# Where the four packed transposes of a gated attention layer land in PSUM: a change of bank and of order

## The chip, the cores and the metric

The kernel runs on one core of a Trainium2 chip. The metric is device time in microseconds (us) of one execution, as the median of several runs. The core's engines run side by side and meet only at semaphores: TensorE (PE in the profile; PEld are its weight loads), VectorE (DVE), ScalarE (ACT), GpSimd (POOL) and SyncE (SP), which only issues transfers here. PSUM has eight banks of 128 x 512 float32; PE writes its results there, DVE and ACT read them.

## The reference

The layer has two halves. The first convolves outer products of a context with a kernel of taps and multiplies with the normalised input; the second is a gated linear attention with two experts per head. Cut to what matters:

```
kv  = einsum('bhil,bhjl->bijhl', ctx, ctx)
out = causal_conv(kv, ssm_kernel) + kv * D
x   = x + tanh(g0) * einsum('bijhl,bhil->bjhl', out, layernorm(x))

y = silu(y_prev * conv_w[:, 0] + y * conv_w[:, 1])      # y = layernorm(x)
q, k, v, g = silu(y @ Wq), y @ Wk, y @ Wv, y @ Wg        # rotary on q and k
q_exp = q * masked_scores * norm ; k_exp = k * onehot    # router from v
o = normalise(tril(q_exp @ k_exp.T) @ v)
x = x + tanh(g1) * (silu(g) * o) @ Wout
```

Shapes: x is (16, 256, 512), float32; 16 heads in the attention.

## The kernel before, in words

The 256 rows of x are cut into 32 groups (`NH`) of 128 rows (8 channels of 16 batches). A Python loop, fully unrolled, runs steps `h = -2 .. 32`. In one step three groups are in flight: `pre` prepares group h+2 (context products `kv` on POOL, their high parts on ACT at L479, their low parts on POOL at L629), `front` convolves group h+1 (`conv`, `conv_last`, then `add_transposed` at L276, 32 transposes that sum `z_terms` into bank 2, from which DVE makes `x2` at L855 and its statistics), `back` projects group h (q, k, logits, v, gate), and `tail` finishes the group whose `back` ran one step earlier (attention output, gate, output projection). Matrix products are made in three passes from a high and a low part of each operand. `back` runs in 32 steps, h = 0 to 31; `tail` in h = 1 to 32; `front` ends with h = 30.

There is no scheduler: the order on each engine is the order in which its block is written, and every hand-over is a `wait_ge` on a semaphore. The part around the change, in PE's order within a step: the v projection into bank 4 (L406); `add_transposed` into bank 2 (L410); the four transposes of `gated` into bank 7 (L415); the gate's projection into bank 5 (L419); the eight transposes of `qke`, k's half into bank 5 (L422) and q's half into bank 3 (L423); the output projection into bank 6 (L432); the scores (L347), which write banks 2, 4, 5 and 3; and, at the head of the next step, the transposes of `z` into bank 7 (L356).

Who reads these banks: ACT applies SiLU to the gate out of bank 5 (L583, `gate_sb`), and copies `gatedT_high` out of bank 7 (L577), k out of bank 5 (L597, `keT`) and q out of bank 3 (L600, `qeT`). DVE makes `gatedT_low` out of bank 7 (L870), behind the chain of `x2` (L855 to L866) in its own order. The layer norm's `rstd2` is made on POOL (L635) and used by ACT for `z` (L590), which stands ahead of the copies of k and q in ACT's order.

Because k's half goes into the bank from which the gate is still to be read, PE waits for `gate_ready` ahead of L422.

Of the kernel before, what the change touches and what calls it, by code (L numbers as in the profile page):

```python
# [13 lines left out]
P = 128  # L14
# [15 lines left out]
def flamingo_gated_layer(nc, x, ctx_t, g_xattn, g_ffn, ssm_kernel, ssm_D, conv_w, Wq, Wk, Wv, Wg,  # L30
# [14 lines left out]
    CH = L // P  # L45
# [20 lines left out]
    with ExitStack() as stack:  # L66
# [195 lines left out]
        def _(eng):  # L262
# [59 lines left out]
            def step(t, p, q, tail, back, front, pre):  # L322
# [14 lines left out]
                def scores():  # L337

                    eng.wait_ge(keT_sb, h + 1)
                    eng.wait_ge(qeT_sb, h + 1)  # L340
                    if front:
# [10 lines left out]
                if back:  # L352
                    eng.wait_ge(z_ready, h + 1)
                    if can_wait(h - 1):
                        eng.wait_ge(gatedT_ready, h - 1)
                    transpose4(bank[7], lambda c: z[:, c * P:(c + 1) * P], zT_ps)  # L356
# [46 lines left out]
                if back:  # L403
                    if can_wait(h):
                        eng.wait_ge(o_normed, h)
                    project(bank[4], yT_p, w_all_p, V0, DV, v_ps, y_low, h + 1)  # L406
                if front:
                    if pre:
                        eng.wait_ge(qx_ready, h + 3)
                    add_transposed(h + 1)  # L410
                if tail:
                    eng.wait_ge(gated_ready, h)
                    if back:
                        eng.wait_ge(y_conv, h + 1)
                    transpose4(bank[7], lambda c: gated[:, c * P:(c + 1) * P], gatedT_ps)  # L415
                if back:
                    if can_wait(h):
                        eng.wait_ge(mask_done[2], h)
                    project(bank[5], yT_p, w_all_p, G0, DV, g_ps, y_low, h + 1)  # L419
                    eng.wait_ge(qke_ready, h + 1)  # L420
                    eng.wait_ge(gate_ready, h + 1)
                    transpose4(bank[5], lambda c: qke[:, RH + 4 * c:RH + 4 * c + 4, :], keT_ps)  # L422
                    transpose4(bank[3], lambda c: qke[:, 4 * c:4 * c + 4, :], qeT_ps)  # L423
                if tail:
                    if isinstance(h, int) and h == 1:
# [13 lines left out]
        def _(eng):  # L439
# [41 lines left out]
            def step(t, p, q, tail, back, front, pre):  # L481
# [83 lines left out]
                if back:  # L565
# [3 lines left out]
                    eng.activation(v_sb[:, :], bank[4][:, :], ACT.Copy).then_inc(v_copied, 1)  # L569
                if pre:  # L570
                    kv_round(p, 2, h + 2)
                    kv_round(p, 3, h + 2)
                if tail:
                    eng.wait_ge(gatedT_ps, h)
                    if can_wait(h - 1):
                        eng.wait_ge(out_ps, h - 1)
                    eng.activation(gatedT_p[0][:, :, :], bank[7][:, :].rearrange("p (c n) -> p c n", c=CH), ACT.Copy  # L577
                                   ).then_inc(gatedT_high, 1)
                if back:
                    eng.wait_ge(g_ps, h + 1)  # L580
# [11 lines left out]
                if back:  # L592
                    eng.wait_ge(keT_ps, h + 1)
                    if can_wait(h):
                        for r in range(CH):
                            eng.wait_ge(attn_ps[r], h)
                    eng.activation(keT[:, :, :], bank[5][:, :].rearrange("p (c n) -> p c n", c=CH), ACT.Copy  # L597
                                   ).then_inc(keT_sb, 1)
                    eng.wait_ge(qeT_ps, h + 1)
                    eng.activation(qeT[:, :, :], bank[3][:, :].rearrange("p (c n) -> p c n", c=CH), ACT.Copy  # L600
                                   ).then_inc(qeT_sb, 1)

            run(eng, step)
# [333 lines left out]
```

## Time and profile before

| | us |
|---|---|
| three runs: lowest, median, highest | 1014.01, 1015.58, 1015.77 |
| the profiled execution's own time | 1016.0 |
| its span, first to last instruction | 1014.2 |
| PE busy in it | 930.4 |
| DVE, ACT, POOL busy | 627.9, 426.9, 672.9 |
| mean granted TensorE clock | 0.981 |

The span is shorter than the execution's time by 1.8 us, which lie around it. A matmul in the timeline is drawn with its modelled duration, which overlaps the next one; the distance between the starts is what PE spends on it. A weight load overlaps the matmul ahead. In a row of the timeline the bracket at the end gives the idle time ahead of the group and who ended it.

### The profile page before, as it was taken

The page shows a single profiled execution, that of the slowest core. Times are in us where ns is not written, and L with a number is a line of the kernel's source. Part 1 is how long each engine was busy: PE and PEld are TensorE (multiplying, and loading weights), DVE is VectorE, ACT ScalarE, POOL GpSimd, SP SyncE. Part 2 cuts the span into 40 slices and gives each one's busy share as a digit, 9 for nine tenths or more (in the row PEclk, how much of TensorE's full clock was granted, in tenths as well). Part 3 has the DMA queues.
Part 4 walks back from the last instruction along what each step waited for, and adds up shares of the span by engine and source line. Part 5 has one row for each costly group of instructions (what it writes and reads, how often), then busy time and mean ns, then how long its engine had stood idle before and what let it go on. Part 6 is the DMA issues. An engine that isn't in the chain of part 4 may idle for free.

```text
span 1014.2 us, 18862 instructions
## 1 busy us (share of the span) xinstructions
PE 930.4 (92%) x7168; PEld 790.7 (78%) x7168; DVE 627.9 (62%) x1400; ACT 426.9 (42%) x906; POOL 672.9 (66%) x613
## 2 busy tenths in 40 slices
PE   1599999999999999999999999999999999999983
PEld 1488888888888888888888888888888878888862
DVE  4766666657666665666666567666656756656542
ACT  2454444444444444434444443444444444444220
POOL 6677667777666677766667776666777666676321
PEclk9889999999999999999999999999999999999986
DMA  8101222112222210222221022222101222210000
GB/s 275 59 30 44 58 58 58 28 31 58 59 58 58 58 32 28 57 59 58 58 58 32 28 57 59 58 59 58 37 24 56 58 59 58 58 37 9 9 12 21
DMA packets 25992, 52.50 MB, mean 52 GB/s; under 512 B 2544, under 2 KB 3696, under 8 KB 25904
## 3 DMA queue, kind: packets, MB, share of 16 engines
q1 hardware_dynamic: 22304, 46.59, 17.1%
q10 hardware_dynamic: 3600, 4.72, 1.4%
q8 instruction: 57, 0.93, 0.4%
q14 instruction: 31, 0.25, 0.1%
HBM read 42.75 MB, written 8.55 MB: 51 GB/s over the span
## 4 chain that ended last, share of the span: by engine, by line
PE 81%; DMA 5%; issue 4%; POOL 4%; DVE 3%; ACT 2%; SPq 0%; POOLq 0%; ACTq 0%
PE bank L315 34%; PE bank L289 19%; PE bank L276 10%; PE bank L265 8%; DMA x_in<-in_x 4%; PE bank L301 3%; PE bank L347 3%; PE bank L333 3%; ACT gate_sb L583 2%; POOL o_rstd L635 1%; DMA w_all<-in_L_ffn_Wv 1%; POOL rstd L635 1%; POOL rot_b L658 1%; DVE gated L827 0%; POOL kv_low L629 0%
## 5 line engine op out<-in xcount | busy, mean ns | idle before, releaser
L629 POOL TENSOR_TENSOR kv_low<-kv,kv_high 128x576 fp32r<-128x576 f32 x128 | 182.0, 1433 | 162.2 <-ACT kv_high L479 162.2
L289 PE MATMUL bank<-kv_high,toep 128*128 128x512 f32 x640 | 225.2, 409 | 11.0 <-DVE z_terms L732 5.6
L620 POOL TENSOR_TENSOR kv<-kx 128x512 f32<-128x512 f32 x128 | 159.2, 1244 | 6.7 <-DMA const<-shape_consts 6.7
L289 PEld LDWEIGHTS bank<-kv_high,toep 128*128 128x128 f32 x640 | 123.0, 192 | 42.1 <-DVE z_terms L732 12.1
L635 POOL TENSOR_TENSOR o_rstd<-o_ve,minus_half 128x16 f32<-128x16 f32 x32 | 93.1, 2911 | 81.7 <-DVE o_ve L802 81.7
L479 ACT ACTIVATE kv_high<-kv 128x576 fp32r<-128x576 f32 x128 | 87.6, 687 | 101.8 <-POOL kv L623 101.8
L289 PE MATMUL bank<-kv_low,toep 128*128 128x512 f32 x320 | 127.4, 398 | 0.0
L315 PE MATMUL bank<-w_all_high,yT_high 128*128 128x512 f32 (+2 forms) x512 | 120.5, 357 | 1.8 <-DVE gated L827 1.8
L880 DVE TENSOR_TENSOR out_sb<-bank,x 128x512 f32<-128x512 f32 x32 | 22.1, 692 | 159.0 <-PE bank L315 159.0
L276 PEld LDWEIGHTS bank<-const,z_terms 128*128 128x128 f32 x1024 | 113.8, 141 | 5.5 <-ACT qx L468 1.2
L276 PE MATMUL bank<-const,z_terms 128*128 128x128 f32 x1024 | 117.0, 273 | 1.0 <-ACT qx L468 1.0
L315 PE MATMUL bank<-w_all_low,yT_high 128*128 128x512 f32 (+2 forms) x512 | 112.7, 342 | 0.0
L315 PE MATMUL bank<-w_all_high,yT_low 128*128 128x512 f32 (+2 forms) x512 | 106.7, 341 | 0.0
L742 DVE TENSOR_TENSOR qke<-rot_a,sel 128x1024 f32<-128x1024 f32 x32 | 69.1, 2158 | 38.8 <-POOL rot_a L661 38.8
L315 PEld LDWEIGHTS bank<-w_all_low,yT_high 128*128 128x128 f32 x512 | 84.4, 190 | 11.1
L315 PEld LDWEIGHTS bank<-w_all_high,yT_low 128*128 128x128 f32 x512 | 81.7, 190 | 11.6
L737 DVE TENSOR_TENSOR att<-bank,const 128x512 f32<-128x512 f32 x128 | 79.5, 684 | 17.8 <-PE bank L347 17.8
L728 DVE TENSOR_TENSOR z_terms<-bank,qx 128x512 f32<-128x512 f32 x128 | 85.4, 667 | 4.5 <-PE bank L289 4.5
L315 PEld LDWEIGHTS bank<-w_all_high,yT_high 128*128 128x128 f32 x512 | 79.2, 191 | 9.0 <-DVE gated L827 3.1
L635 POOL TENSOR_TENSOR rstd<-ve,minus_half 128x1 f32<-128x1 f32 x64 | 36.6, 572 | 69.0 <-DVE ve L793 60.4
L495 ACT ACTIVATE y_raw<-bank,w_conv 128x128 f32<-128x128 f32 x128 | 36.6, 370 | 95.7 <-PE bank L265 95.7
L623 POOL TENSOR_TENSOR kv<-kx 128x64 f32<-128x64 f32 x128 | 73.1, 571 | 0.0
(101 smaller groups left out, 1650.5 us busy)
## 6 DMA issues: line engine op xcount, KB each, us to landing
toep<-taps_dram SPq DMA_DIRECT2D x32, 512.0 KB, 7.1
kx<-in_ctx SPq DMA_DIRECT2D x32, 384.0 KB, 7.5
x_in<-in_x SPq DMA_DIRECT2D x32, 256.0 KB
out_x<-out_sb SPq DMA_DIRECT2D x32, 256.0 KB
w_all<-in_L_ffn_Wv ACTq DMA_DIRECT2D x1, 1024.0 KB, 12.6
w_all<-in_L_ffn_Wg ACTq DMA_DIRECT2D x1, 1024.0 KB, 11.3
w_out<-in_L_ffn_Wout ACTq DMA_DIRECT2D x1, 1024.0 KB, 17.1
router<-in_L_ffn_router_w ACTq DMA_DIRECT2D x1, 512.0 KB, 7.3
```

Source lines behind the costliest of these rows:

```text
L265: ins = nc.tensor.transpose(dst[:, c * P:(c + 1) * P], src(c), ident)
L276: ins = nc.tensor.matmul(bank[2][:, c * P:(c + 1) * P], z_terms[:, c, i * ROW:(i + 1) * ROW], ident, is_transpose=True, start=(c == 0 and ...
L289: ins = nc.tensor.matmul(bank[lc % 2][:, :], toep[:, 1 - p, a, (lc - mc) * P:(lc - mc + 1) * P], kv_p[b][:, 1 - p, mc, 0:FULL], start=(mc ...
L315: ins = nc.tensor.matmul(dst[:, 0:cols], src_p[a][:, c, :], w_p[b][:, c, c0:c0 + cols], start=(i == 0 and c == 0), stop=(i == len(PASSES) ...
L479: eng.activation(kv_p[0][:, p, c, :], kv[:, c % 2, :], ACT.Copy).then_inc(kv_high[c], 1)
L620: eng.tensor_tensor(view(kv[:, c % 2, 0:FULL], [[ROW, NROT], [1, ROW]]), view(kx[:, p, c, 0:ROW], [[0, NROT], [1, ROW]]), view(kx[:, p, c, ...
L623: eng.tensor_tensor(kv[:, c % 2, FULL:FULL + HALF], kx[:, p, c, 0:HALF], kx[:, p, c, HALF:2 * HALF], ALU.mult).then_inc(kv_made[c], 1)
L629: eng.tensor_tensor(kv_p[1][:, p, c, :], kv[:, c % 2, :], kv_p[0][:, p, c, :].bitcast(F32), ALU.subtract).then_inc(kv_ready[c], 1)
L635: eng.tensor_tensor(dst[:, 0:n], src[:, 0:n], minus_half[:, 0:n], ALU.pow).then_inc(done, 1)
L728: eng.tensor_tensor(view(z_terms[:, lc, 0:1], [[ROW, NROT], [1, ROW]]), view(y[:, 0:1], [[ROW, NROT], [1, ROW]]), view(q, [[NB, NROT], [1, ...
L737: eng.tensor_tensor(att[:, r, :, :], bank[SCORE_BANKS[r]][:, :].rearrange("p (c n) -> p c n", c=CH), view(mask[:, 0:1], [[0, CH], [1, P]]) ...
L742: eng.tensor_tensor(view(qke[:, 0, 0:1], [[RATIO * HDK, 2 * RH], [HDK, RATIO], [1, HDK]]), view(rot_a[:, 0, 0:1], [[HDK, 2 * RH], [0, RATI ...
```

## The change

The transposes of k go into bank 7 instead of bank 5. PE does the transposes of `gated` ahead of `add_transposed`, and those of q ahead of those of k. The wait for `gate_ready` moves from the transposes to the scores (which write bank 5); in its old place stands nothing for q, and for k a wait for `gatedT_ready`, after which bank 7 has been read out. The transposes of `z` now wait for `keT_sb` of the step before. ACT copies `gatedT_high` ahead of its last two rounds of `kv_high`, and q ahead of k. No instruction is added or taken away.

```diff
@@ PE @@
                 def scores():
+                    eng.wait_ge(qeT_sb, h + 1)
                     eng.wait_ge(keT_sb, h + 1)
-                    eng.wait_ge(qeT_sb, h + 1)
+                    eng.wait_ge(gate_ready, h + 1)
...
                 if back:
                     eng.wait_ge(z_ready, h + 1)
-                    if can_wait(h - 1):
-                        eng.wait_ge(gatedT_ready, h - 1)
+                    if can_wait(h):
+                        eng.wait_ge(keT_sb, h)
                     transpose4(bank[7], lambda c: z[:, c * P:(c + 1) * P], zT_ps)
...
                     project(bank[4], yT_p, w_all_p, V0, DV, v_ps, y_low, h + 1)
+                if tail:
+                    eng.wait_ge(gated_ready, h)
+                    if back:
+                        eng.wait_ge(y_conv, h + 1)
+                    else:
+                        eng.wait_ge(keT_sb, h)
+                    transpose4(bank[7], lambda c: gated[:, c * P:(c + 1) * P], gatedT_ps)
                 if front:
                     if pre:
                         eng.wait_ge(qx_ready, h + 3)
                     add_transposed(h + 1)
-                if tail:
-                    eng.wait_ge(gated_ready, h)
-                    if back:
-                        eng.wait_ge(y_conv, h + 1)
-                    transpose4(bank[7], lambda c: gated[:, c * P:(c + 1) * P], gatedT_ps)
                 if back:
                     if can_wait(h):
                         eng.wait_ge(mask_done[2], h)
                     project(bank[5], yT_p, w_all_p, G0, DV, g_ps, y_low, h + 1)
                     eng.wait_ge(qke_ready, h + 1)
-                    eng.wait_ge(gate_ready, h + 1)
-                    transpose4(bank[5], lambda c: qke[:, RH + 4 * c:RH + 4 * c + 4, :], keT_ps)
                     transpose4(bank[3], lambda c: qke[:, 4 * c:4 * c + 4, :], qeT_ps)
+                    if tail:
+                        eng.wait_ge(gatedT_ready, h)
+                    transpose4(bank[7], lambda c: qke[:, RH + 4 * c:RH + 4 * c + 4, :], keT_ps)
@@ ACT @@
                     eng.activation(v_sb[:, :], bank[4][:, :], ACT.Copy).then_inc(v_copied, 1)
-                if pre:
-                    kv_round(p, 2, h + 2)
-                    kv_round(p, 3, h + 2)
                 if tail:
                     eng.wait_ge(gatedT_ps, h)
...
                     eng.activation(gatedT_p[0][:, :, :], bank[7][:, :].rearrange("p (c n) -> p c n", c=CH), ACT.Copy
                                    ).then_inc(gatedT_high, 1)
+                if pre:
+                    kv_round(p, 2, h + 2)
+                    kv_round(p, 3, h + 2)
```

ACT's last two copies change places in the same way (q's wait for the scores' last reads moves with it).

PE, step h = 1, from the end of the v projection to the scores, before:

```order
L315 MATMUL bank<-w_all_high,yT_low 128x512 x4
L276 MATMUL bank<-const,z_terms 128x128 x32
L265 MATMUL bank<-const,gated 128x128 x4
L315 MATMUL bank<-w_all_high,yT_high 128x512 x4
L315 MATMUL bank<-w_all_low,yT_high 128x512 x4
L315 MATMUL bank<-w_all_high,yT_low 128x512 x4
L265 MATMUL bank<-const,qke 128x128 x8
L315 MATMUL bank<-w_out_high,gatedT_high 128x512 x4
```

and now:

```order
L315 MATMUL bank<-w_all_high,yT_low 128x512 x4
L265 MATMUL bank<-const,gated 128x128 x4
L276 MATMUL bank<-const,z_terms 128x128 x32
L315 MATMUL bank<-w_all_high,yT_high 128x512 x4
L315 MATMUL bank<-w_all_low,yT_high 128x512 x4
L315 MATMUL bank<-w_all_high,yT_low 128x512 x4
L265 MATMUL bank<-const,qke 128x128 x8
L315 MATMUL bank<-w_out_high,gatedT_high 128x512 x4
```

The four transposes of `gated` have passed the 32 of `z_terms`; the eight of `qke` stand where they stood, q's four now first.

PE, the same step, with the waits in brackets, from the transposes of `qke` to those of `z`, before:

```order
L265 MATMUL bank<-const,qke 128x128 [waits gate_ready,qke_ready]
L265 MATMUL bank<-const,qke 128x128 x7
L315 MATMUL bank<-w_out_high,gatedT_high 128x512 [waits ratio_ready,gatedT_high,w_ready]
L315 MATMUL bank<-w_out_high,gatedT_high 128x512 x3
L315 MATMUL bank<-w_out_low,gatedT_high 128x512 x4
L315 MATMUL bank<-w_out_high,gatedT_low 128x512 [waits gatedT_ready]
L315 MATMUL bank<-w_out_high,gatedT_low 128x512 x3
L347 MATMUL bank<-qeT,keT 128x128 [waits x2_ready,v_copied,qeT_sb,keT_sb]
L347 MATMUL bank<-qeT,keT 128x128 x15
L265 MATMUL bank<-const,z 128x128 [waits gatedT_ready,z_ready]
```

and now:

```order
L265 MATMUL bank<-const,qke 128x128 [waits qke_ready]
L265 MATMUL bank<-const,qke 128x128 x3
L265 MATMUL bank<-const,qke 128x128 [waits gatedT_ready]
L265 MATMUL bank<-const,qke 128x128 x3
L315 MATMUL bank<-w_out_high,gatedT_high 128x512 [waits ratio_ready,gatedT_high,w_ready]
L315 MATMUL bank<-w_out_high,gatedT_high 128x512 x3
L315 MATMUL bank<-w_out_low,gatedT_high 128x512 x4
L315 MATMUL bank<-w_out_high,gatedT_low 128x512 [waits gatedT_ready]
L315 MATMUL bank<-w_out_high,gatedT_low 128x512 x3
L348 MATMUL bank<-qeT,keT 128x128 [waits x2_ready,gate_ready,v_copied,keT_sb,qeT_sb]
L348 MATMUL bank<-qeT,keT 128x128 x15
L265 MATMUL bank<-const,z 128x128 [waits keT_sb,z_ready]
```

The wait for the gate has gone to the scores, and the wait for `gatedT_ready` stands in the middle of the eight transposes.

ACT, the same step, from the copy of v to the last copy, before:

```order
L569 ACTIVATE v_sb<-bank 128x512 [waits oT_ps,v_ps]
L479 ACTIVATE kv_high<-kv 128x576 [waits conv_last_ps,conv_ps3,kv_made2]
L479 ACTIVATE kv_high<-kv 128x576 [waits conv_last_ps,conv_ps3,kv_made3]
L577 ACTIVATE gatedT_high<-bank 128x512 [waits gatedT_ps]
L583 ACTIVATE gate_sb<-bank 128x512 [waits gated_ready,g_ps]
L586 ACTIVATE nmr<-nmu,rstd 128x1 [waits rstd2_ready]
L590 ACTIVATE z<-x,nmr,rstd 128x512 [waits nmr2_ready,zT_ps]
L597 ACTIVATE keT<-bank 128x512 [waits attn_ps2,attn_ps1,attn_ps3,attn_ps0,keT_ps]
L600 ACTIVATE qeT<-bank 128x512 [waits qeT_ps]
```

and now:

```order
L573 ACTIVATE v_sb<-bank 128x512 [waits oT_ps,v_ps]
L578 ACTIVATE gatedT_high<-bank 128x512 [waits gatedT_ps]
L483 ACTIVATE kv_high<-kv 128x576 [waits conv_last_ps,conv_ps3,kv_made2]
L483 ACTIVATE kv_high<-kv 128x576 [waits conv_last_ps,conv_ps3,kv_made3]
L587 ACTIVATE gate_sb<-bank 128x512 [waits gated_ready,g_ps]
L590 ACTIVATE nmr<-nmu,rstd 128x1 [waits rstd2_ready]
L594 ACTIVATE z<-x,nmr,rstd 128x512 [waits nmr2_ready,zT_ps]
L601 ACTIVATE qeT<-bank 128x512 [waits attn_ps2,attn_ps1,attn_ps3,attn_ps0,qeT_ps]
L604 ACTIVATE keT<-bank 128x512 [waits keT_ps]
```

`gatedT_high` has passed two rounds of `kv_high`, and the copy of k is the last of the step. The orders of DVE, POOL and SP are what they were.

## Rows read from the trace of the kernel before

**Rows 1.** The page: busy us (share of the span) and instructions of each engine.
```profile
PE 930.4 (92%) x7168; PEld 790.7 (78%) x7168; DVE 627.9 (62%) x1400; ACT 426.9 (42%) x906; POOL 672.9 (66%) x613
```

**Rows 2.** Waits of PE: line <- releaser: us in total, times, longest us.
```profile
PE bank L265 <- ACT gate_sb L583: 24.9, 32, 0.8
```

**Rows 3.** Timeline of PE in one middle step: start, us, instruction, count [idle before].
```profile
509.61 1.10 PE L315 MATMUL bank<-w_all_high,yT_low 128*128 128x512 f32 x4
510.54 3.66 PE L276 MATMUL bank<-const,z_terms 128*128 128x128 f32 x32
514.03 0.60 PE L265 MATMUL bank<-const,gated 128*128 128x128 f32 x4
514.39 1.17 PE L315 MATMUL bank<-w_all_high,yT_high 128*128 128x512 f32 x4
...
516.33 1.09 PE L315 MATMUL bank<-w_all_high,yT_low 128*128 128x512 f32 x4
518.21 1.06 PE L265 MATMUL bank<-const,qke 128*128 128x128 f32 x8 [0.78 <-ACT gate_sb L583]
519.02 1.17 PE L315 MATMUL bank<-w_out_high,gatedT_high 128*128 128x512 f32 x4
...
521.96 1.17 PE L347 MATMUL bank<-qeT,keT 32*128 32x128 f32 x32
```

**Rows 4.** Timeline of ACT in the same step.
```profile
513.77 0.68 ACT L479 ACTIVATE kv_high<-kv 128x576 fp32r<-128x576 f32 x1 [2.43 <-POOL kv L623]
...
517.46 0.60 ACT L583 ACTIVATE gate_sb<-bank 128x512 f32<-128x512 f32 x1 [1.06 <-PE bank L315]
...
518.90 0.82 ACT L590 ACTIVATE z<-x,nmr,rstd 128x512 f32<-128x512 f32 x1
519.63 0.58 ACT L597 ACTIVATE keT<-bank 128x512 f32<-128x512 f32 x1
520.10 0.59 ACT L600 ACTIVATE qeT<-bank 128x512 f32<-128x512 f32 x1
523.75 1.15 ACT L495 ACTIVATE y_raw<-bank,w_conv 128x128 f32<-128x128 f32 x4 [3.06 <-PE bank L265]
```

**Rows 5.** Timeline of DVE in the same step.
```profile
507.62 1.04 DVE L832 TENSOR_TENSOR gated<-gated,gate_sb 128x512 f32<-128x512 f32 x1
...
511.34 2.22 DVE L742 TENSOR_TENSOR qke<-rot_a,sel 128x1024 f32<-128x1024 f32 x1 [1.23 <-POOL rot_a L661]
514.24 0.75 DVE L855 SCALAR_TENSOR_TENSOR x<-bank,gates,x_in 128x512 f32<-128x512 f32 x1 [0.68 <-PE bank L276]
...
516.04 0.14 DVE L866 TENSOR_SCALAR ve<-mv 128x1 f32<-128x1 f32 x1
516.44 0.69 DVE L870 TENSOR_TENSOR gatedT_low<-bank,gatedT_high 128x512 fp32r<-128x512 f32 x1 [0.25 <-ACT gatedT_high L577]
522.06 0.69 DVE L880 TENSOR_TENSOR out_sb<-bank,x 128x512 f32<-128x512 f32 x1 [4.93 <-PE bank L315]
```

**Rows 6.** Timeline of POOL in the same step.
```profile
517.94 0.54 POOL L635 TENSOR_TENSOR rstd<-ve,minus_half 128x1 f32<-128x1 f32 x1
...
525.55 1.42 POOL L629 TENSOR_TENSOR kv_low<-kv,kv_high 128x576 fp32r<-128x576 f32 x1 [4.12 <-ACT kv_high L479]
```

**Rows 7.** Timeline of step h = 0: last copy on ACT, scores on PE.
```profile
78.39 0.59 ACT L600 ACTIVATE qeT<-bank 128x512 f32<-128x512 f32 x1
79.08 1.17 PE L347 MATMUL bank<-qeT,keT 32*128 32x128 f32 x32 [1.80 <-ACT keT L597]
```

**Rows 8.** Timeline of step h = 31 and the last: DVE, and PE behind DVE.
```profile
980.82 1.23 DVE L742 TENSOR_TENSOR qke<-rot_a,sel 128x1024 f32<-128x1024 f32 x1 [2.03 <-POOL rot_a L661]
...
989.40 2.49 DVE L737 TENSOR_TENSOR att<-bank,const 128x512 f32<-128x512 f32 x4 [0.39 <-PE bank L347]
...
992.15 1.68 PE L333 MATMUL bank<-att,v_sb 128*32 128x128 f32 x32 [2.76 <-DVE att L737]
```

**Rows 9.** Busy time by stretch: length, PE, PEld, DVE, ACT, POOL, PE's clock, DMA.
```profile
492.90:522.30 29.40, 28.53 (x235) 24.36 (x231) 18.89 (x44) 12.92 (x28) 20.80 (x19) 1.00 0.20 50
```

More of the change, by code:

```diff
@@ L592, in step @@
                 if back:
-                    eng.wait_ge(keT_ps, h + 1)
+                    eng.wait_ge(qeT_ps, h + 1)
                     if can_wait(h):
@@ L596, in step @@
                             eng.wait_ge(attn_ps[r], h)
-                    eng.activation(keT[:, :, :], bank[5][:, :].rearrange("p (c n) -> p c n", c=CH), ACT.Copy
-                                   ).then_inc(keT_sb, 1)
-                    eng.wait_ge(qeT_ps, h + 1)
                     eng.activation(qeT[:, :, :], bank[3][:, :].rearrange("p (c n) -> p c n", c=CH), ACT.Copy
                                    ).then_inc(qeT_sb, 1)
+                    eng.wait_ge(keT_ps, h + 1)
+                    eng.activation(keT[:, :, :], bank[7][:, :].rearrange("p (c n) -> p c n", c=CH), ACT.Copy
+                                   ).then_inc(keT_sb, 1)
             run(eng, step)
```

## The prediction, made before the changed kernel had run

> **What bounds the kernel now.** I read the page's busy times first, then PE's waits, then one middle step in the timeline of each engine, and last the first and last steps. The page has PE busy for 92% of the span, DVE and POOL for about two thirds [rows 1]: PE is the engine to ask about. Its waits have one entry that comes back in every step: the transposes of `qke` wait for the gate's SiLU on ACT, 32 times, 24.9 us in all, 0.78 us each [rows 2]. All that precedes it within the step runs on PE without a pause.
>
> The 0.78 us is what remains behind the modelled end of the last matmul. What PE really loses is longer. Four matmuls of 128x512 take 0.93 us from start to start (509.61 to 510.54), so the gate's last four, begun at 516.33, would have let the next instruction start at 517.26. It started at 518.21: **0.95 us lost per step** [rows 3]. In between ACT ran `gate_sb` from 517.46 to 518.06 and PE followed 0.15 us later [rows 4]. The other input of these transposes, `qke`, was ready at 511.34 + 2.22 = 513.56 [rows 5]. So the wait for the gate alone makes the pause, and it is there only because k's transposes write the gate's bank.
>
> **The change part by part.** All positions are in the time of the step shown, as if PE had not yet been shifted.
>
> *The wait for the gate goes from the transposes.* Removed: 0.95 us per `back` step. The gate is awaited at the scores instead; it is ready at 518.06, and the scores would start no earlier than 521.96 - 0.95 = 521.01. Almost 3 us of output projection cover it; I cost it at nothing.
>
> *Transposes of `gated` ahead of `add_transposed`.* They start at 510.54; `gated` is finished at 507.62 + 1.04 = 508.66, 1.88 us earlier, so no wait. They take 0.36 us (514.03 to 514.39), which `add_transposed` is now later; the gate's projection still starts at 514.39 [rows 3, 5]. PE's sum is unchanged. Queued behind `add_transposed` is DVE's `x2` chain: it starts at 514.60 instead of 514.24, and its last step, begun at 516.04 for 0.14 us, ends at 516.54 instead of 516.18. POOL takes up its `rstd` only at 517.94, behind its own `kv_low`, so 1.40 us of slack swallow the 0.36 and `z` does not move [rows 5, 6]. SP waits for `x2_ready` ahead of the next load of `x_in`, which is due a whole step later.
>
> *The new wait for `gatedT_ready` ahead of k's transposes.* Queued behind it on PE: k's transposes, the output projection and the scores, so any lateness is paid in full. ACT's copy of `gatedT_high` now falls into the 2.43 us in which ACT was idle ahead of the `kv_high` round of 513.77: it costs ACT nothing [rows 4]. DVE, which had waited 0.25 us for it, starts `gatedT_low` straight behind the `x2` chain at 516.54, ends at 517.23. A real hand-over from DVE to PE takes 992.15 - (989.40 + 2.49) = 0.26 us [rows 8], so k's transposes may start at 517.49. PE asks for them at 517.26 plus four transposes: the eight take 0.81 us (518.21 to 519.02), four 0.36 to 0.41. That is 517.62 to 517.67 [rows 3]. **Slack 0.13 to 0.18 us; cost nothing**, but thin.
>
> *q's copy first, k's last.* ACT's last copy still ends at 520.10 + 0.59 = 520.69, since both copies stand behind `z` (518.90 to 519.72), which POOL's `rstd` releases [rows 4, 6]. k's transposes are done by about 518.1, so ACT does not wait for them. In step 0 the hand-over from this last copy to the scores took 79.08 - 78.98 = 0.10 us [rows 7]; behind the gate it was 0.15. The scores may start at 520.79 to 520.84; PE now asks at 521.01. **Slack about 0.2 us; cost nothing.** This is what becomes late next: the copies do not move while PE does, and of 1.1 us of slack 0.2 remain.
>
> The Trainium skill (ScalarE: Activation LUTs, What ACT_TABLE_LOAD costs) puts a copy of 512 elements at 186 ns + 0.833 ns an element, with 93 ns of overlap, an estimate of 0.52 us from start to start. The rows have 0.47 (519.63 to 520.10) [rows 4]; by the page the last copy would end about 0.1 us later and half of this slack be gone, and the sum would still be the same.
>
> *`z`'s transposes wait for `keT_sb` instead of an older `gatedT_ready`.* The scores just ahead have waited for the same value. Nothing.
>
> *The other engines in the shortened step.* Each of them stood still for PE after the pause: DVE 4.93 us ahead of `out_sb`, ACT 3.06 ahead of `y_raw`, POOL 4.12 ahead of `kv_low` [rows 4 to 6]. Taking off 0.95 leaves all three waiting, so the next step finds the same distances, and the gain comes again in each.
>
> *One place is shared.* POOL and DVE run side by side here, and a DVE instruction can be stretched: `qke` takes 2.22 us in the middle step, beside POOL, and 1.23 in step 31 with POOL idle [rows 5, 8]. Its place beside POOL doesn't move, since POOL's `rot_a` releases it. The pieces that move by 0.36 us are the `x2` chain and `gatedT_low`, beside POOL's `kv_low` as before. Bounds for `gatedT_low`: its own 0.69, or stretched as `qke` is, 0.69 x 2.22 / 1.23 = 1.25, which would use up the slack and cost 0.4 us a step. I take 0.69, measured beside the same neighbour.
>
> The Trainium skill (SBUF — State Buffer, SBUF: two separate sides) says why the two cases could differ: DVE locks POOL out, or is locked out, where it reads two inputs from SBUF, and `gatedT_low` reads one of its two from PSUM. By the opposite case, a stretch for any DVE work beside POOL, the sum would be 12 us smaller; the 0.69 us of the middle step speaks for the rule.
>
> *Where it does not count.* In step 0 there is no output projection between transposes and scores: PE waited 1.80 us for the copies there, and they end when they did [rows 7]. That step gives nothing. Steps 1 to 31 do; 31 has neither `z` nor `x2` in the way. Some of the clock below full speed lies in the first and last 50 us; the middle step has it at 1.00 with the pause in it [rows 9], so I expect no gain or loss of clock.
>
> **Sum:** 31 x 0.95 = 29.4 us. Against the profiled execution: span 1014.2 to 984.8, time 1016.0 to 986.6. Against the median of the runs, 1015.58, which lies 0.4 below that execution: **986.1 us**. Small things around it: q's and k's transposes no longer start from a standstill and may take 0.72 instead of 0.81 us (up to 3 us less); the split by a wait, and the fifth wait at the scores, may cost some hundredths (up to 2 us more). So 983 to 988.5 for this case.
>
> **The rivals.**
>
> *A. One of the thin slacks is gone.* k's copy or `gatedT_low` arrives 0.1 to 0.4 us after PE asks. For it: 0.13 to 0.2 us are hardly more than a hand-over, and I put together times of different engines. Against it: both estimates already hold the longest hand-over that the rows show or nearly so. Price: 3 to 12 us, 989 to 998; likeliest 0.15 us a step, 991.
>
> *B. Slower: `gatedT_low` becomes the bound.* It stands behind the whole `x2` chain, which the change puts 0.36 us later, and behind it PE now holds three things. From 1.12 us of lateness on (0.95 gained plus 0.17 of slack) the step is longer than before. If the chain were stretched by 1.5 us, each step would lose 0.38: 31 x 0.38 = 12 us, 1027. Against it: the chain runs beside the same POOL work as now, and DVE waits for nothing else in it.
>
> *C. The pause stays.* PE is held at that place by something else than the gate, or the edit only moves the wait from the transposes to the scores. Then 1015. For it: the wait is put down to one semaphore of two. Against it: `qke` was ready 3.7 us before the gate's projection ended.
>
> *D. More than forecast,* below 983: a pause that the modelled ends hide elsewhere closes too. I see none that the change touches.
>
> **How the numbers follow.** Forecast 0.76; A 0.14; B 0.03; C 0.04; D 0.03. 986.1 is the forecast's. The range reaches from 983 over the forecast's own bounds into the likelier half of A, to 993; it leaves out D, B, C and the rest of A, some 0.15. About 0.2% (2 us) is what a measurement can tell from no change. Faster by more than that are the forecast, A and D, 0.93; same C, 0.04; slower B, 0.03.
>
> **What would show it.** In PE's waits the entry for `gate_sb` is gone, save perhaps once in step 0. The distance from the gate's last four matmuls to the first transpose of `qke` is 0.93 us and not 1.88. `gatedT_low` starts right behind the `x2` chain with no idle time ahead. ACT's last copy ends 0.3 us ahead of the scores. If A holds, PE has some 30 small waits at the scores for `keT`, or in the middle of the `qke` transposes for `gatedT_low`. If the step is not 0.95 us shorter while the gate's wait is gone, the rule that the other engines only follow PE is wrong.

## The result, and the profile after

The changed kernel takes **985.54 us** (median of 4 runs, 984.67 to 987.3) against 1015.29 for the kernel before, beside which it ran (4 runs, 1014.01 to 1015.77). The ratio is 0.9711, with a 95% interval of 0.9698 to 0.9723. On another chip it was 985.29 against 1015.23. The prediction was 986.1.

The page of the changed kernel, its first lines (span, then busy us, share of the span and instructions of each engine):

```profile
span 984.4 us, 18833 instructions
PE 923.5 (94%) x7168; PEld 792.4 (81%) x7168; DVE 624.8 (63%) x1400; ACT 426.9 (43%) x906; POOL 673.0 (68%) x613
```

The work is what it was [rows 1], 29.8 us are gone from the span, and no engine's share changed by more than two points, PE's weight loads apart, which went from 78 to 81%. The waits of PE (line <- releaser: us in total, times, longest) of the changed kernel, from the longest:

```profile
PE bank L265 <- ACT qn L562: 15.7, 1, 15.7
...
PE bank L315 <- DVE gated L831: 3.0, 6, 1.5
PE bank L348 <- ACT keT L604: 2.8, 1, 2.8
```

The entry for `gate_sb`, 24.9 us in 32 pieces [rows 2], doesn't exist any more. What is left comes once or twice, at the start or the end, except one entry of six pieces for `gated`, to which I come back. (Lines behind the edits have moved by one on PE and by four on the others: L347 is now L348, L870 is L874.)

One middle step of the changed kernel in the timeline, PE:

```profile
496.06 1.09 PE L315 MATMUL bank<-w_all_high,yT_low 128*128 128x512 f32 x4
496.99 0.60 PE L265 MATMUL bank<-const,gated 128*128 128x128 f32 x4
497.43 3.66 PE L276 MATMUL bank<-const,z_terms 128*128 128x128 f32 x32
500.84 1.18 PE L315 MATMUL bank<-w_all_high,yT_high 128*128 128x512 f32 x4
...
502.78 1.08 PE L315 MATMUL bank<-w_all_high,yT_low 128*128 128x512 f32 x4
503.70 1.03 PE L265 MATMUL bank<-const,qke 128*128 128x128 f32 x8
504.49 1.16 PE L315 MATMUL bank<-w_out_high,gatedT_high 128*128 128x512 f32 x4
...
507.42 1.17 PE L348 MATMUL bank<-qeT,keT 32*128 32x128 f32 x32
```

From the gate's last four matmuls to the transposes of `qke` it is 0.92 us now (502.78 to 503.70), where it was 1.88 [rows 3]: the pause is gone, whole. ACT and DVE in the same step:

```profile
497.68 0.59 ACT L578 ACTIVATE gatedT_high<-bank 128x512 fp32r<-128x512 f32 x1
...
503.90 0.60 ACT L587 ACTIVATE gate_sb<-bank 128x512 f32<-128x512 f32 x1 [1.53 <-PE bank L315]
...
506.56 0.59 ACT L604 ACTIVATE keT<-bank 128x512 f32<-128x512 f32 x1
```

```profile
501.12 0.75 DVE L859 SCALAR_TENSOR_TENSOR x<-bank,gates,x_in 128x512 f32<-128x512 f32 x1 [1.12 <-PE bank L276]
...
502.98 0.68 DVE L874 TENSOR_TENSOR gatedT_low<-bank,gatedT_high 128x512 fp32r<-128x512 f32 x1
```

PE has gone into `qke` at 503.70 while ACT is still to run the gate's SiLU (503.90 to 504.50). `gatedT_low` follows the `x2` chain without idle time and ends at 503.66; ACT's last copy ends at 507.15, 0.27 us ahead of the scores.

**Where the 29.8 us came from.** The starts of the scores divide both traces. From the first instruction to the scores of h = 1: 108.58 before, 107.26 after, 1.3 us; the pause of step 1 stood in this stretch, since it comes ahead of the step's scores. From there to the scores of h = 30: 855.26 (108.58 to 963.84) and 827.45 (107.26 to 934.71), 27.8 us or 0.96 in each of 29 steps. From h = 30 to h = 31: 24.37 and 23.63, 0.7 us. Behind it: 25.99 and 26.06.

### The profile page after: what moved, and what is told of

It is laid out like the page before. It is cut to its first block, busy times and chain, and to the rows that moved or that the text cites. A ratio compares the mean times of both kernels' runs of the same rounds, so it can differ in the third digit from the quotient of the medians.

```text
span 984.4 us, 18833 instructions
## 1 busy us (share of the span) xinstructions
PE 923.5 (94%) x7168; PEld 792.4 (81%) x7168; DVE 624.8 (63%) x1400; ACT 426.9 (43%) x906; POOL 673.0 (68%) x613
## 4 chain that ended last, share of the span: by engine, by line
PE 81%; DMA 5%; issue 5%; POOL 4%; DVE 3%; ACT 1%; SPq 0%; POOLq 0%; ACTq 0%
PE bank L315 33%; PE bank L289 19%; PE bank L276 11%; PE bank L265 8%; DMA x_in<-in_x 4%; PE bank L301 4%; PE bank L348 3%; PE bank L333 3%; POOL o_rstd L639 2%; DMA w_all<-in_L_ffn_Wv 1%; POOL rstd L639 1%; POOL rot_b L662 1%; POOL kv_low L633 0%; DVE gated L831 0%; DVE out_sb L884 0%
## 5 line engine op out<-in xcount | busy, mean ns | idle before, releaser
L736 DVE TENSOR_TENSOR z_terms<-bank,qx 128x384 f32<-128x384 f32 x128 | 69.8, 545 | 0.0
```

The lines of the kernel that those rows point to most:

```text
L736: eng.tensor_tensor(view(z_terms[:, lc, first:first + 1], [[ROW + NB, NROT - 1], [1, ROW]]), view(y[:, ROW:ROW + 1], [[ROW, NROT - 1], [1, ...
```

## Experiments

Four of them take the change apart, two idle instructions put a price on its thin slacks, and the rest follow what they showed. All were timed beside the kernel before on the same chip, which lay at 1015.2 to 1016.3.

### The wait alone, put back

```diff
                     eng.wait_ge(qke_ready, h + 1)
+                    eng.wait_ge(gate_ready, h + 1)
                     transpose4(bank[3], lambda c: qke[:, 4 * c:4 * c + 4, :], qeT_ps)
```

> The changed kernel with one line more: PE waits for gate_ready ahead of q's transposes, as before the change. Bank, order of the transposes and order of the copies stay changed. Theory (the gain is this wait and nothing else): the gate's SiLU pause of 0.95 us comes back in steps 1 to 31, about 29 us, and the time is 1013 to 1016; in PE's waits 32 entries of 0.78 us for gate_sb. Rival (part of the gain is the new order): the time stays clearly below 1012.

Measured: 1014.52 us (10 runs, 1013.25 to 1016.31), ratio 0.9991 (0.9981 to 1.0). The waits of PE have the old line back, to the tenth:

```profile
PE bank L265 <- ACT gate_sb L588: 24.9, 32, 0.8
```

Bank and order of the changed kernel, and the whole gain is gone. The gain is this wait. What was moved around it is worth 0.9 us by the ratio, 1.5 by the medians (1016.0 for the kernel before beside it), and hardly anything in the middle steps: from the scores of h = 1 to those of h = 30 it is 854.98 us, against 855.26 in the kernel before.

### The bank alone

The kernel before with the three edits that the new bank needs, and q ahead of k; nothing of `gated` is moved, neither on PE nor on ACT.

```diff
                     eng.wait_ge(qke_ready, h + 1)
-                    eng.wait_ge(gate_ready, h + 1)
-                    transpose4(bank[5], lambda c: qke[:, RH + 4 * c:RH + 4 * c + 4, :], keT_ps)
                     transpose4(bank[3], lambda c: qke[:, 4 * c:4 * c + 4, :], qeT_ps)
+                    if tail:
+                        eng.wait_ge(gatedT_ready, h)
+                    transpose4(bank[7], lambda c: qke[:, RH + 4 * c:RH + 4 * c + 4, :], keT_ps)
```

> The kernel before with k's transposes in bank 7 and q's ahead of k's, the gate awaited at the scores; the transposes of gated stay behind add_transposed, and ACT copies gatedT_high behind its kv_high rounds as before. Theory (only the bank counts, gatedT_low is just in time): in the trace of before gatedT_low ended at 517.13, so k's transposes may start at 517.39 with a hand-over of 0.26; PE asks for them at 517.26 + 0.40 = 517.66. No wait, 985 to 988, as the changed kernel. Rival (the two moves are needed to get gatedT_low out in time): 0.1 to 0.3 us a step lost in the middle of the qke transposes, 989 to 995.

Measured: 985.67 us (983.95 to 986.2), ratio 0.9701 (0.9686 to 0.9715): the changed kernel's time. DVE and PE of this kernel around the place:

```profile
502.53 0.69 DVE L874 TENSOR_TENSOR gatedT_low<-bank,gatedT_high 128x512 fp32r<-128x512 f32 x1 [0.26 <-ACT gatedT_high L581]
```

```profile
502.42 1.08 PE L315 MATMUL bank<-w_all_high,yT_low 128*128 128x512 f32 x4
503.34 1.03 PE L265 MATMUL bank<-const,qke 128*128 128x128 f32 x8
504.13 1.16 PE L315 MATMUL bank<-w_out_high,gatedT_high 128*128 128x512 f32 x4
```

`gatedT_low` ends at 503.22, before even q's transposes begin. The earlier copy of `gatedT_high` would take away the 0.26 us of idle time on DVE, the later `add_transposed` adds 0.36 to the chain ahead: the two moves nearly cancel (`gatedT_low` ends 0.80 us behind the start of the gate's last four matmuls here and 0.88 in the changed kernel), and neither was needed.

### The same, k ahead of q

```diff
                     eng.wait_ge(qke_ready, h + 1)
+                    if tail:
+                        eng.wait_ge(gatedT_ready, h)
+                    transpose4(bank[7], lambda c: qke[:, RH + 4 * c:RH + 4 * c + 4, :], keT_ps)
                     transpose4(bank[3], lambda c: qke[:, 4 * c:4 * c + 4, :], qeT_ps)
-                    if tail:
-                        eng.wait_ge(gatedT_ready, h)
-                    transpose4(bank[7], lambda c: qke[:, RH + 4 * c:RH + 4 * c + 4, :], keT_ps)
```

> As bank_only, but k's transposes ahead of q's, as in the kernel before. Now PE asks for bank 7 at 517.26, 0.13 us before gatedT_low can be handed over (517.39). Theory (slack by these rows): 31 x 0.13 = 4 us more than bank_only, 989 to 992, and PE stands in front of the qke transposes for gatedT_low. Rival (a hand-over is shorter, as the 0.05 us at another place of the trace): no difference from bank_only.

Measured: 986.80 us (985.13 to 987.81), ratio 0.9713 (0.9698 to 0.9728). Theory missed, rival nearly right: 1.1 us more than the bank alone, not 4.

```profile
503.48 0.69 DVE L874 TENSOR_TENSOR gatedT_low<-bank,gatedT_high 128x512 fp32r<-128x512 f32 x1 [0.25 <-ACT gatedT_high L581]
```

```profile
503.38 1.09 PE L315 MATMUL bank<-w_all_high,yT_low 128*128 128x512 f32 x4
504.31 1.06 PE L265 MATMUL bank<-const,qke 128*128 128x128 f32 x8
505.13 1.18 PE L315 MATMUL bank<-w_out_high,gatedT_high 128*128 128x512 f32 x4
```

k's transposes start at 504.31, 0.93 us behind the gate's last four matmuls, 0.14 behind the end of `gatedT_low` (504.17). So this hand-over takes 0.14 us or less, and not the 0.26 on which I had built the slack. The eight transposes take 0.82 instead of 0.79, the start ahead of them 0.93 instead of 0.92: 31 x 0.04 = 1.2 us, the measured difference, though it is within the spread of the runs.

### q first, in the old bank

```diff
                     eng.wait_ge(qke_ready, h + 1)
-                    eng.wait_ge(gate_ready, h + 1)
-                    transpose4(bank[5], lambda c: qke[:, RH + 4 * c:RH + 4 * c + 4, :], keT_ps)
                     transpose4(bank[3], lambda c: qke[:, 4 * c:4 * c + 4, :], qeT_ps)
+                    eng.wait_ge(gate_ready, h + 1)
+                    transpose4(bank[5], lambda c: qke[:, RH + 4 * c:RH + 4 * c + 4, :], keT_ps)
```

(ACT's copies of q and k change places with them.)

> The kernel before with q's transposes ahead of the wait for the gate and k's behind it, still in the gate's bank 5; ACT copies q first. Nothing else moved. Theory: q's four transposes (0.36 to 0.41 us) fill a part of the 0.95 us pause, so 31 x 0.38 = 12 us are gained, 1003 to 1004. Rival (the pause is a restart cost of PE that any wait brings): gain under 5 us, above 1010.

Measured: 999.45 us (998.92 to 1000.65), ratio 0.9841 (0.9827 to 0.9856). PE and ACT:

```profile
509.13 1.08 PE L315 MATMUL bank<-w_all_high,yT_low 128*128 128x512 f32 x4
510.05 0.60 PE L265 MATMUL bank<-const,qke 128*128 128x128 f32 x4
510.90 0.66 PE L265 MATMUL bank<-const,qke 128*128 128x128 f32 x4 [0.25 <-ACT gate_sb L583]
511.32 1.16 PE L315 MATMUL bank<-w_out_high,gatedT_high 128*128 128x512 f32 x4
```

```profile
510.25 0.60 ACT L583 ACTIVATE gate_sb<-bank 128x512 f32<-128x512 f32 x1 [1.05 <-PE bank L315]
```

Exchanging the two halves on PE and on ACT, in the old bank, brings more than half of the gain. The direction was as expected, the size was not: 2.19 us from the gate's last matmuls to the output projection (509.13 to 511.32) against 2.69 before [rows 3], 0.50 a step and not 0.38. q's four fill about 0.40. The other 0.10 is the hand-over: k's transposes start 0.05 us behind the end of `gate_sb` (510.85), where it had been 0.15. PE had stood for 0.25 us there, and for 0.78 in the kernel before; why the shorter pause goes with the shorter hand-over is not shown. 31 x 0.50 = 15.5 of the 16.5 us measured. That also answers this experiment's rival: the wait is still there 32 times, and costs what ACT is late, not a fixed sum.

### How thin is the slack at the scores

The changed kernel once more as the base, and the same with one idle copy on ACT:

```diff
+                    eng.activation(view(pad[:, 0:1], [[P, 3], [1, P]]), view(ident[:, 0:1], [[0, 3], [1, P]]), ACT.Copy)
                     eng.activation(qeT[:, :, :], bank[3][:, :].rearrange("p (c n) -> p c n", c=CH), ACT.Copy
```

> The changed kernel itself, on the same chip as the three beside it, as the base of their comparison. 984.5 to 987.

> The changed kernel with one idle copy more on ACT (384 columns into a tile that nobody reads) ahead of the copies of q and k. In the trace of after ACT's last copy ends 0.27 us ahead of the scores' start, with a hand-over of 0.05 to 0.15 us. The pad takes about 0.10 + 384/512 x 0.42 = 0.42 us, so the last copy comes 0.20 to 0.30 us late. Theory (this slack is what remains, and it is thin): 31 x 0.2 to 0.3 = 6 to 9 us slower than after_again, 992 to 995, with some 30 waits of PE for keT at the scores. Rival (the slack is larger than these rows say, or the copies would move forward with PE): within 2 us of after_again.

Measured: 985.29 us (984.73 to 987.1), ratio 0.9707 (0.9693 to 0.9721); with the pad 990.09 (990.0 to 990.19), ratio 0.9752 (0.9740 to 0.9765). ACT and PE with the pad:

```profile
508.50 0.51 ACT L602 ACTIVATE pad<-const 128x384 f32<-128x384 f32 x1
508.91 0.58 ACT L603 ACTIVATE qeT<-bank 128x512 f32<-128x512 f32 x1
509.39 0.59 ACT L606 ACTIVATE keT<-bank 128x512 f32<-128x512 f32 x1
```

```profile
508.93 1.08 PE L316 MATMUL bank<-w_out_high,gatedT_low 128*128 128x512 f32 x4
510.07 1.17 PE L349 MATMUL bank<-qeT,keT 32*128 32x128 f32 x32
```

The pad delays the copies by 0.41 us (508.50 to 508.91). In this step the scores come 1.14 us behind the output projection's last four instead of 1.02, so 0.12 of it is paid. The page's waits show nothing of this, since 0.12 us hides behind the modelled end of the matmul ahead.

The slack is not the difference of 0.29, because in PE's time the copies did not come 0.41 us later. POOL's `rstd`, from which `z` and the copies follow, in the changed kernel, and with the pad beside the gate's last four matmuls:

```profile
504.38 0.56 POOL L639 TENSOR_TENSOR rstd<-ve,minus_half 128x1 f32<-128x1 f32 x1
```

```profile
505.31 1.08 PE L316 MATMUL bank<-w_all_high,yT_low 128*128 128x512 f32 x4
506.80 0.55 POOL L641 TENSOR_TENSOR rstd<-ve,minus_half 128x1 f32<-128x1 f32 x1
```

Counted from the start of the gate's last four, `rstd` starts at 1.60 us in the changed kernel (504.38 - 502.78) and at 1.49 with the pad, and the last copy ends at 4.37 and at 4.67. So the copies are 0.30 us later, of which 0.18 was slack: the 0.27 us of the changed kernel less a hand-over of 0.09 (509.98 to 510.07). The other steps agree. In all of steps 1 to 29 of the padded kernel the scores follow the last copy by 0.09 to 0.11 us, and from the transposes of `qke` to the scores it is 3.83 to 3.96 us, where the changed kernel has 3.71 to 3.74: PE does wait for `keT` in each. How much of a wait it is varies with `rstd`, which starts a little earlier or later in each; why it does, I have not followed.

From the scores of h = 1 to those of h = 30 it is 830.09 us (108.99 to 939.08) against the changed kernel's 827.45, 2.6 us; the rest of the 4.8 lies at the ends, in step 0 above all, where the scores wait 3.21 us instead of 2.78. The theory's mechanism held, and so did its slack. Its price of 6 to 9 us was too high: a usual step is 28.55 us instead of 28.45, so it grows by less than what is paid ahead of the scores. About 0.03 us of that comes back at `attention_output`; where the rest does, I have not followed.

### ACT's copies ahead of z

```diff
-                if front:
-                    eng.wait_ge(rstd2_ready, h + 2)
...
                 if back:
                     eng.wait_ge(qeT_ps, h + 1)
...
                                    ).then_inc(keT_sb, 1)
+                if front:
+                    eng.wait_ge(rstd2_ready, h + 2)
```

> The changed kernel with ACT's copies of q and k ahead of its nmr and z instead of behind them. Nothing else moves. Theory (the copies end late only because z, which waits for POOL's rstd, stands ahead): in middle steps the last copy ends about 1.6 us earlier and nothing is gained there, since PE did not wait; in step 0 the scores' wait of 2.8 us shrinks to about 0.9, and with it the stretch at half clock behind it goes. 2 to 3 us faster than after_again: 982.5 to 983.5. Rival (step 0 is held by another chain, POOL's or the loads): same as after_again.

Measured: 981.85 us (981.59 to 983.32), ratio 0.9674 (0.9661 to 0.9687), against 985.29 for the changed kernel on the same chip; on another chip it gave 981.60 (ratio 0.9665). Step 0 of the changed kernel, and of this one:

```profile
76.74 0.59 ACT L604 ACTIVATE keT<-bank 128x512 f32<-128x512 f32 x1
77.42 1.96 PE L348 MATMUL bank<-qeT,keT 32*128 32x128 f32 x32 [2.78 <-ACT keT L604]
```

```profile
75.30 0.60 ACT L596 ACTIVATE keT<-bank 128x512 f32<-128x512 f32 x1
76.00 1.17 PE L348 MATMUL bank<-qeT,keT 32*128 32x128 f32 x32 [0.84 <-ACT keT L596]
```

The scores of h = 1 start at 104.44 instead of 107.26 (106.98 in the base's trace); from there to h = 30 it is 827.31 us, as in the changed kernel. In the traces the whole gain lies in step 0, as expected: 2.5 us against the base. The medians differ by 3.4 us, a little more than the 2 to 3 expected, and the traces do not show where the other 0.9 lies. In the changed kernel's profile PE's granted clock was 0.72 of full speed from 76 to 82 us, behind that wait of 2.78 us, and the scores took 1.96 us instead of 1.17; from the scores of h = 0 to those of h = 1 it was 29.84 us. In the base's trace, with the same wait, the clock stayed at 1.00, the scores took 1.17 us and the step 28.43. So the half clock behind the pause comes in some executions and not in others.

This version is faster than both kernels. What is the slack at the scores in it?

> z_last once more, on the same chip as the three beside it, as the base of two of them. 981 to 983.

> z_last with the same idle copy of 384 columns (0.41 us from start to start in act_pad3's trace) ahead of the copies of q and k. In act_pad3 it cost 4.8 us and a step 0.11 us longer. Theory (the slack at the scores was thin only because the copies stood behind z): in z_last the last copy ends 504.00 - (501.45 + 0.61) = 1.94 us ahead of the scores, so 0.41 us more costs nothing in steps 1 to 31, and about 0.4 in step 0: within 1 us of z_last_again. Rival (what act_pad3 lost was ACT's time in the loop, not lateness at the scores): again 3 to 5 us slower.

Measured: 981.60 us (981.32 to 982.72), and 983.12 (982.61 to 983.25) with the pad. From h = 1 to h = 30 the padded kernel takes 826.82 us (105.60 to 932.42), no more than without it; in step 0 its scores wait 1.25 us instead of 0.84. The same 0.41 us on ACT cost 2.6 us in the middle steps of `act_pad3` and nothing here. So it was lateness at the scores, and the place of `z` had made it. The 1.5 us between the medians are more than the 1 us expected and more than step 0's 0.4 explains. In the traces another 0.4 lies ahead of that wait (the scores of h = 0 start at 77.12 instead of 76.29); I leave the rest open.

### How thin is the slack at gatedT_low

```diff
+                    eng.tensor_scalar(view(pad[:, 0:1], [[P, 3], [1, P]]), view(ident[:, 0:1], [[0, 3], [1, P]]), 1.0, None, ALU.mult)
                     eng.tensor_tensor(gatedT_p[1][:, :, :], bank[7][:, :].rearrange("p (c n) -> p c n", c=CH),
```

> The changed kernel with one idle instruction on DVE (384 columns, SBUF to SBUF, into a tile that nobody reads) ahead of gatedT_low, behind the x2 chain. It takes 0.25 to 0.45 us. In the trace of after gatedT_low ends at 503.66 and k's transposes start about 0.40 us behind 503.70, so the slack is 0.44 us less a hand-over; bank_k_first bore 0.14 us from end to start without a wait, which leaves 0.30. Theory (what the prediction feared in its rival B, with the corrected hand-over): 0 to 0.15 us a step, 0 to 5 us slower than after_again's 985.3. Rival (hand-over 0.26 as the prediction took it): 0.1 to 0.3 us a step, 3 to 9 us.

Measured: 986.09 us (985.56 to 988.12), ratio 0.9710 (0.9694 to 0.9725). The changed kernel's ratios were 0.9711 and 0.9707, on other chips: no difference that the runs can tell.

```profile
504.15 0.54 DVE L875 TENSOR_SCALAR pad<-const 128x384 f32<-128x384 f32 x1
504.61 0.68 DVE L876 TENSOR_TENSOR gatedT_low<-bank,gatedT_high 128x512 fp32r<-128x512 f32 x1
```

```profile
504.86 1.14 PE L266 MATMUL bank<-const,qke 128*128 128x128 f32 x8
505.76 1.16 PE L316 MATMUL bank<-w_out_high,gatedT_high 128*128 128x512 f32 x4
```

`gatedT_low` came 0.46 us late, and the eight transposes took 0.90 us instead of 0.79: 0.11 paid, 0.35 borne. The weight load of k's first transpose starts at 505.34, 0.05 us behind the end of `gatedT_low` (505.29). The theory with the corrected hand-over holds for the step. It does not give the total: a usual step did grow from 28.45 to 28.55 us, which would be 3 us, but from h = 1 to h = 30 it is 828.83 us against 827.45, because only two of its steps are over 28.75 us where the changed kernel has five (more on them below). For rival B of the prediction to decide, the chain would have had to be 0.35 + 0.95 = 1.3 us late.

### The wait that the page doesn't show

> z_last, and besides the scores ahead of the last of the three passes of the output projection, with DVE's four masks ahead of out_sb. Reason: in the changed kernel attention_output starts 511.35 where the convolution ahead of it lets go at 510.86 + 0.23 = 511.09, which is when DVE's last mask ends: a hidden wait of 0.26 us a step that the page doesn't count. Theory: the masks come about 1 us earlier, the 0.26 us go in steps 1 to 30, 8 us: 974 to 976. Rival (the 0.26 us is what PE needs anyway to change to these small tiles): no gain over z_last.

```diff
-                    project(bank[6], gatedT_p, w_out_p, 0, L, out_ps, gatedT_ready, h)
+                    project(bank[6], gatedT_p, w_out_p, 0, L, out_ps, gatedT_ready, h, passes=(0, 1))
                 if back:
                     scores()
+                if tail:
+                    project(bank[6], gatedT_p, w_out_p, 0, L, out_ps, gatedT_ready, h, passes=(2,))
```

Measured: 1079.55 us, the median of six runs that spread from 1061.35 to 1085.43. The ratio of 1.0505 (1.0462 to 1.0549) goes by the two shortest, 1061.35 and 1071.73: 5% slower than the kernel before. The trace is of the longest. Both theory and rival had missed the mechanism. DVE's waits, and SP's issues in one step:

```profile
DVE stats L791 <- DMA x_in<-in_x: 82.9, 29, 6.6
```

```profile
529.96 0.67 SPq L255 DMA_DIRECT2D out_x<-out_sb  x1
530.67 0.60 SPq L242 DMA_DIRECT2D x_in<-in_x  x1
```

SP is one queue. It waits for `out_sb` ahead of the store, and the next load of `x_in` stands behind the store. DVE's four masks ahead of `out_sb` made that wait 2.4 us longer; the load came late in 29 steps, DVE stood for it, and PE for `gated` behind DVE (54.4 us in 29 pieces). A part of the loss is clock: most steps here take 32.2 to 34.0 us, and four take 30.9 to 31.0. In one of the former the granted clock is 0.50 from 639 to 642 us, behind pauses of PE of 0.23 and 1.89 us; in one of the four, to which the two rows of SP belong, it is 1.00 throughout. I had read PE's and DVE's order for this edit, and not SP's. With the load ahead of the store:

```diff
                         eng.dma_start(x_in[:, p, :], xg[h + 2]).then_inc(s_x[p], 16)
+                        if h > 1:
+                            store(h - 1, 1 - p)
```

(`store` is the wait for `out_ready` and the store of a group; the end of the loop issues the last ones.)

> scores_early with one order more changed: SP issues a step's load of x_in ahead of the store of the step before. In scores_early DVE's out_sb, now behind the masks, became ready 2.4 us later; SP, which waits for it ahead of the next x_in, issued that load late, DVE stood 2.59 us for x_in, and PE 1.9 us behind it for gated. Theory (that queue is the whole loss, and the hidden 0.26 us ahead of attention_output is a real wait): 30 x 0.17 us are gained over z_last (in scores_early the attention started 0.09 us behind the convolution instead of 0.26), about 5 us: 976 to 978. Rival (another thing in scores_early is slow too): above 982.

Measured: **971.46 us** (970.88 to 974.45), ratio 0.9568 (0.9550 to 0.9585). That is 10 us below z_last, twice what I expected. PE ahead of `attention_output`, in the changed kernel and in this one:

```profile
510.86 0.40 PE L289 MATMUL bank<-kv_high,toep 128*128 128x512 f32 x1
511.35 1.08 PE L333 MATMUL bank<-att,v_sb 128*32 128x128 f32 x32
```

```profile
503.93 0.39 PE L296 MATMUL bank<-kv_high,toep 128*128 128x512 f32 x1
504.25 1.08 PE L340 MATMUL bank<-att,v_sb 128*32 128x128 f32 x32
```

The distance is 0.49 us and then 0.32, so 0.17 of it was a wait for DVE's last mask. A usual step is 28.26 us from scores to scores against 28.45 (28.44 in z_last's second trace). The rest is something I had not looked for. In the changed kernel five of the steps are 0.5 us longer than the others (29.01, 29.0, 29.1, 28.92, 28.94), and the kernel before has the same five. In one of them, DVE and PE:

```profile
201.52 0.69 DVE L789 BATCH_NORM_STATS2 stats<-x_in 128x6 f32<-128x512 f32 x1 [0.58 <-DMA x_in<-in_x]
207.57 0.69 DVE L831 TENSOR_TENSOR gated<-bank,o_rstd 128x512 f32<-128x512 f32 x1 [2.04 <-POOL o_rstd L639]
208.32 1.19 PE L315 MATMUL bank<-w_all_high,yT_high 128*128 128x512 f32 x4 [0.33 <-DVE gated L831]
```

The same load, issued behind the store, lands too late now and then: here it was issued at 194.17 and DVE had it at 201.52, 7.35 us later, while the next one, issued at 223.18, was there when DVE came for it at 229.88. Why the transfer takes longer in some steps is not shown. These are five of the six pieces among PE's waits, 1.5 us together; the sixth, of 1.5 us, comes at the end. With the load issued first only that one is left, of 1.4 us, and the middle steps of the last kernel lie between 28.25 and 28.27. Against z_last on the same chip it is 819.15 us from h = 1 to h = 30 instead of 826.90, 7.75 us: 29 x 0.18 = 5.2 for all steps, and about 0.5 more for each of the five long ones. The remaining 2 us of the medians' difference lie at the ends (the scores of h = 1 start at 103.89 instead of 104.72, and h = 30 to h = 31 takes 22.69 us instead of 23.44), and I have not followed them. No run has the load ahead of the store and nothing else, so what each of the two edits gives is read from the traces and not shown by a run of its own.

## Why the prediction was right, point by point

*The gate's wait, 0.95 us a step.* Right. A usual step went from 29.4 to 28.45 us, and with the wait put back (`wait_back`) it is 29.4 again. Counting from start to start was what gave the size: the page's 0.78 us a step would have made 24 us.

*31 steps.* Right in sum, not in each. Steps 2 to 30 gave 27.8 us and step 31 only 0.7. Step 1's share lies in the 1.3 us ahead of its scores: from the scores of h = 0 to those of h = 1 it was 29.50 us before and 28.43 in the base's trace, 1.07 less, and 29.84 in the changed kernel's first trace, where the stretch at half clock took it back. The scores of h = 0 moved only with what lay ahead of them, from 79.08 to 77.42, and the base's trace has them at 78.55. I had said that step 0 gives nothing, and had not said that PE's pause there grows from 1.80 to 2.78 us, behind which the clock may fall to its lower level of 1.2 GHz.

*The number.* 986.1 against 985.54. The step is understood to some hundredths of a us; that the medians meet within 0.6 is in part luck, as single runs spread over 2.6 us and the half clock of step 0 takes 1.4 in some of them. Of the small terms, the transposes of `qke` without a standstill took 0.79 us and not the 0.72 that I thought possible, 0.6 us in all instead of 3.

*`gated` ahead of `add_transposed`.* Costs nothing, as said. The four transposes take 0.44 instead of 0.36 us there and the 32 behind them 3.41 instead of 3.49: the sum is the same. It also brings nothing, which the prediction did not see: it took the slack of the changed order and never asked for that of the old one.

*The slack for k's transposes, 0.13 to 0.18 us.* The place was right, the size not. The 0.26 us hand-over was read where PE stood still and then began small tiles; at a transpose in a running queue it is at most 0.14. The slack was 0.35. So k's transposes were never close to waiting.

*The slack at the scores, about 0.2 us.* Right. In steps 1 to 29 of the changed kernel the last copy ends 0.26 to 0.39 us ahead of the scores, 0.30 on average, and the hand-over is 0.10 in the padded kernel's steps. The chain behind it was right too: POOL's `rstd`, then `z`, then the copies.

*`gatedT_low` not stretched.* Right, 0.68 us, as 0.69 before. The Trainium skill (SBUF — State Buffer, SBUF: two separate sides) has DVE and POOL lock each other out where DVE reads two inputs from SBUF; `gatedT_low` reads one from PSUM, and its 0.68 us beside POOL's `kv_low` agrees with that. No run here tests the rule itself.

*The rivals.* A, B and C did not occur. A's mechanism exists: it sets in when the copies come about 0.2 us later, or `gatedT_low` 0.35. D did not occur either. The modelled ends do hide a pause, the one ahead of `attention_output`, but the change does not touch it.

## What to carry to other kernels

If an engine waits for another to read a bank, look first for a bank that has been read out already, and then for work of the same engine that can stand ahead of the wait: here the first gave 30 us, the second alone 16. Take a pause from the starts of the matmuls, since the modelled ends hide 0.1 to 0.2 us of each; whole waits can hide there. Before an edit delays a result, read the order of every queue that waits for it, the DMA queue's too: a store that waits holds up the load behind it.

## What the runs showed of the hardware

A hand-over from ACT to PE's transposes took 0.05 us where PE had stood for 0.25 us and 0.15 where it had stood for 0.78, and 0.09 to 0.11 from ACT's last copy to the scores, in 29 steps. From DVE to PE it was at most 0.14 at a transpose (0.05 to the weight load of one, with an idle instruction ahead) and 0.26 ahead of the small tiles of `attention_output`. Eight transposes of 128x128 took 0.81 us behind a wait of PE and 0.79 without one. The wait of 2.8 us in step 0 was followed by a granted clock of 0.50 for 3 us in one execution and by full clock in another; in `scores_early` the same fall came behind pauses of 0.23 and 1.89 us in one step and not in another. Copies of 384 columns on ACT took 0.41 us from start to start, the instruction of 384 columns on DVE 0.46.
